# Softplus in a Mamba scan kernel: the rounding of 1+e moved from GpSimd to ScalarE, and all places in the order set anew

## What is computed

```python
dt = jax.nn.softplus(dbc[..., :DT_RANK] @ dt_proj_w.T + dt_proj_b)
A = -jnp.exp(A_log)
dA = jnp.exp(dt[..., None] * A)
dBu = dt[..., None] * Bm[:, :, None, :] * xs[..., None]
def combine(c1, c2):
    a1, b1 = c1
    a2, b2 = c2
    return (a1 * a2, a2 * b1 + b2)
_, hs = jax.lax.associative_scan(combine, (dA, dBu), axis=1)
y = jnp.einsum('blds,bls->bld', hs, Cm) + xs * Dvec
```

## Time and profile before

| what | value |
|---|---|
| median of 3 runs | 4836.43 us (4832.74 to 4845.68) |
| the profiled execution's own time | 4842.17 us |
| its span, first to last instruction | 4840.4 us |
| mean granted TensorE clock | 0.957 |
| instructions in the trace | 69756 |
| DMA moved | 623.06 MB, mean 129 GB/s |

### The profile page before, as it was taken

How to read it: one execution, slowest core, us unless ns; L and a number is a source line. 1 busy time by engine, 2 the same in 40 slices (tenths; PEclk the granted TensorE clock), 3 DMA queues, 4 the chain that set the end, 5 groups by cost and what they waited for, 6 DMA issues and landing times.

```text
span 4840.4 us, 69756 instructions
## 1 busy us (share of the span) xinstructions
PE 4236.6 (88%) x21206; PEld 1773.4 (37%) x21206; DVE 4002.3 (83%) x5617; ACT 3314.4 (68%) x5382; POOL 3939.5 (81%) x5162
## 2 busy tenths in 40 slices
PE   3578788999999999999989999999999989898897
PEld 1233333333333343434333434343333333333332
DVE  2268889888988888988898989888989898988872
ACT  1356566777777777777767776777777777676665
POOL 1268888888888888888888888888888889898873
PEclk9688899999999999999999999999999999999998
DMA  2366665656555665666656655666665665554430
GB/s 68 79 141 158 145 141 131 143 135 140 136 137 137 140 138 133 138 139 138 141 131 146 141 136 134 139 139 137 140 138 136 145 140 138 132 125 115 95 78 5
DMA packets 255529, 623.06 MB, mean 129 GB/s; under 512 B 105268, under 2 KB 170676, under 8 KB 255028
## 3 DMA queue, kind: packets, MB, share of 16 engines
q1 hardware_dynamic: 255156, 618.60, 55.8%
HBM read 540.85 MB, written 77.65 MB: 128 GB/s over the span
## 4 chain that ended last, share of the span: by engine, by line
POOL 35%; PE 24%; DVE 17%; issue 11%; DMA 7%; ACT 4%; SPq 0%; DVEq 0%; POOLq 0%; ACTq 0%
POOL hc L1156 14%; DVE hs L1011 7%; PE ps L676 5%; DMA dtb<-dt_scratch 5%; DVE ps L1001 4%; PE ps L740 3%; POOL sp L1169 2%; PE ps L689 2%; DVE tmpd L1070 2%; POOL h L1196 2%; POOL yw L1256 2%; PE ps L717 2%; POOL sp L1177 2%; PE ps L800 2%; PE ps L811 2%
## 5 line engine op out<-in xcount | busy, mean ns | idle before, releaser
L1156 POOL TENSOR_TENSOR hc<-hs,cb 128x448 f32<-128x448 f32 x1792 | 2025.6, 1137 | 460.5 <-DVE hs L1011 315.9
L1011 DVE TENSOR_TENSOR_SCAN hs<-dtb,state,ps 128x448 f32<-128x448 f32 x1536 | 1754.7, 1142 | 84.8 <-issue 0.7
L1001 DVE TENSOR_TENSOR ps<-ps,bb 128x448 f32<-128x448 f32 x1792 | 1099.1, 613 | 439.7 <-PE ps L676 437.9
L848 ACT ACTIVATE dtb<-dtb,decay 128x448 f32<-128x448 f32 x1792 | 1092.0, 658 | 156.0 <-DMA dtb<-dt_scratch 154.1
L676 PE MATMUL ps<-dux,pick 128*128 128x448 bf16 x3584 | 1038.1, 371 | 128.7 <-DVE hs L1011 117.1
L890 ACT ACTIVATE hg<-ps,be 128x448 f32<-128x448 f32 x896 | 523.8, 630 | 405.2 <-PE ps L740 404.6
L676 PE MATMUL ps<-duz,pick 128*128 128x448 bf16 x1792 | 642.5, 359 | 0.0
L676 PEld LDWEIGHTS ps<-dux,pick 128*128 128x128 bf16 x3584 | 283.7, 101 | 831.4 <-issue 432.1
L740 PE MATMUL ps<-xn,we 64*128 64x448 f32 x1792 | 564.5, 592 | 7.9 <-ACT hg L890 5.3
L879 ACT ACTIVATE rz<-ps,bnb 128x448 f32<-128x448 f32 x448 | 280.8, 627 | 271.4 <-PE ps L724 271.0
L689 PE MATMUL ps<-hc,gather 128*32 128x448 f32 x3584 | 451.3, 573 | 0.0
(11 more groups left out here) (171 smaller groups left out, 6319.3 us busy)
## 6 DMA issues: line engine op xcount, KB each, us to landing
dtb<-dt_scratch SPq DMA_DIRECT2D x448, 896.0 KB, 6.7
slab<-h_scratch SPq DMA_DIRECT2D x168, 290.0 KB, 8.3
dt_scratch<-sp SPq DMA_DIRECT2D x112, 224.0 KB, 2.0
...
xw<-xn_scratch SPq DMA_DIRECT2D x112, 112.8 KB, 2.7
xw<-xn_scratch SPq DMA_DIRECT2D x112, 112.5 KB, 3.7
```

Of the source, the lines that this page charges most:

```text
L848: A.activation(a, a, ACT.Exp, scale=decay[k % 2][:, i:i + 1]).then_inc(a_ok, 1)
L1001: V.tensor_tensor(bank, bank, bb[:, k % 2, :], ALU.mult).then_inc(bu_ok, 1)
L1011: V.tensor_tensor_scan(rev(hs[:, n % RH, :], d), rev(dtb[i // 4][:, i % 4, :], d), rev(bank, d), state[:, d, i:i + 1] if k % STEPS >= 2 el ...
L1156: P_.tensor_tensor(hc[:, n % 8, :], hs[:, n % RH, :], cb[:, k % 2, :], ALU.mult).then_inc(hc_ok, 1)
```

## The change

(1 + e) - 1 is made on ACT instead of on POOL, in two Identity operations (`lost`): y = 1 + e, and then 1 - y, which is the negative of what `soft_ym` made; `soft_log` adds it. y lies in the second half of dux, which the second part of dt·x overwrites later, so `lost` waits until PE has done with it (bu_ps). `soft_ym` is gone. The semaphore counts of the POOL chain follow. All places are set anew.

```diff
-AHEAD = 6
+AHEAD = 5
...
-'soft_le': -17, 'soft_ym': -17, 'soft_log': -15, 'soft_dt': -14, 'part0': -14, 'part1': -12
+'soft_le': -15, 'lost': -15, 'soft_log': -15, 'soft_dt': -14, 'part0': -9, 'part1': -5
...
+                def lost(kk):
+                    y = dux[:, kk % 2, 1, :]
+                    if kk >= 2:
+                        act.wait_ge(bu_ps, DS * (kk - 1))
+                    act.wait_ge(dt_e, kk + 1)
+                    A.activation(y, sp[:, 0, :], ACT.Identity, bias=1.0).then_inc(dt_y, 1)
+                    act.wait_ge(dt_y, kk + 1)
+                    A.activation(y, y, ACT.Identity, bias=1.0, scale=-1.0).then_inc(dt_r, 1)
...
-                def soft_ym(kk):
-                    pool.wait_ge(sp_ch, 3 * kk + 1)
-                    P_.tensor_scalar(sp[:, 0, :], sp[:, 0, :], 1.0, -1.0, ALU.add, ALU.add).then_inc(sp_ch, 1)
-
                 def soft_log(kk):
-                    pool.wait_ge(sp_ch, 3 * kk + 2)
-                    P_.tensor_tensor(sp[:, 2, :], sp[:, 2, :], sp[:, 0, :], ALU.subtract).then_inc(sp_ch, 1)
+                    pool.wait_ge(sp_ch, 2 * kk + 1)
+                    pool.wait_ge(dt_r, kk + 1)
+                    P_.tensor_tensor(sp[:, 2, :], sp[:, 2, :], dux[:, kk % 2, 1, :], ALU.add).then_inc(sp_ch, 1)
```

More of the change, by code:

```diff
@@ L61 @@
 END = NB * G
-STEP_AT = {'fetch_xw': -27, 'x': -20, 'silu_u': -20, 'dt': -17, 'soft_in': -17, 'bb': -12, 'copy_bb': -11, 'cc': -10, 'copy_cc': -9, 'z': -5, 'soft_le': -17, 'soft_ym': -17, 'soft_log': -15, 'soft_dt': -14, 'part0': -14, 'part1': -12, 'part2': -3, 'put_dt': -10, 'spread0': -5, 'spread1': -2, 'spread2': -2, 'spread3': 1, 'skip': 8, 'gather0': 9, 'gather1': 13, 'gather2': 15, 'gather3': 19, 'gate': 19, 'out_proj': 21, 'add_out': 21}
+STEP_AT = {'fetch_xw': -20, 'x': -20, 'silu_u': -20, 'dt': -17, 'soft_in': -17, 'bb': -12, 'copy_bb': -11, 'cc': -10, 'copy_cc': -9, 'z': -5, 'soft_le': -15, 'lost': -15, 'soft_log': -15, 'soft_dt': -14, 'part0': -9, 'part1': -5, 'part2': -3, 'put_dt': -8, 'spread0': -7, 'spread1': -2, 'spread2': 0, 'spread3': 2, 'skip': 8, 'gather0': 9, 'gather1': 13, 'gather2': 17, 'gather3': 19, 'gate': 19, 'out_proj': 21, 'add_out': 21}
@@ L63 @@
 UP_AT = (0, 0, 1, 1, 2, 2, 3, 3, 8, 8, 9, 9, 10, 10, 11, 11)
[L64 to L69, removed]
@@ L70 @@
-E_AT = {'mean': 1, 'square': 2, 'var': 2, 'power': 4, 'normed': 4, 'tokens_T': 9, 'logits': 10, 'compare': 12, 'places': 13, 'lead': 13, 'ask': 16, 'weigh': 19, 'share': 19, 'weights': 21, 'weight_parts': 21, 'parts': 25, 'fold': 49, 'out': 53}
+DOWN_AT = (4, 7, 12, 15)
+PAIR_AT = (3, 7, 12, 13)
+THIRD_AT = (0, 0, 1, 2, 2, 3, 5, 5, 6, 7, 7, 8, 10, 11, 12, 13)
+FOLD_AT = (4, 6, 7, 9, 11, 11, 14, 14, 14)
+A_AT = {'cut': -15, 'second': -10, 'put0': -10, 'rem1': -9, 'split1': -7, 'put1': -6, 'rem2': -8, 'split2': -6, 'put2': -6, 'arrange': -1, 'x_in': 10, 'paths': 14, 'mean': 16, 'square': 18, 'var': 19, 'power': 19, 'scaled': 20, 'normed': 23, 'norm_T': 24, 'keep_xn': 29}
@@ L71 @@
+F_AT = {'fetch': -4, 'x_T': 3, 'paths_in': 6, 'rows': 10}
+E_AT = {'mean': 0, 'square': 2, 'var': 2, 'power': 2, 'normed': 3, 'tokens_T': 9, 'logits': 10, 'compare': 12, 'places': 13, 'lead': 14, 'ask': 16, 'weigh': 20, 'share': 20, 'weights': 21, 'weight_parts': 21, 'parts': 27, 'fold': 49, 'out': 50}
 EXPERTS = 24
@@ L379, in build @@
         dtb_in = [sem(f"dtb_in{j}") for j in range(4)]
-        dt_e, dt_l, sp_ch, dt_ok, dx_ok = (sem(n) for n in ("dt_e", "dt_l", "sp_ch", "dt_ok", "dx_ok"))
+        dt_e, dt_l, dt_y, dt_r, sp_ch, dt_ok, dx_ok = (sem(n) for n in
+            ("dt_e", "dt_l", "dt_y", "dt_r", "sp_ch", "dt_ok", "dx_ok"))
         bu_ps, bu_ok, a_ok, h_ok, st_ok, hc_ok, y_acc, gated, o_ps, o_rd = (sem(n) for n in
@@ L979, in _ @@
                         soft_in(kk)
+                    for kk in steps_at(n, "lost"):
+                        lost(kk)
             @block.vector
@@ L1265, in _ @@
                         soft_le(kk)
-                    for kk in steps_at(n, "soft_ym"):
-                        soft_ym(kk)
                     for kk in steps_at(n, "soft_log"):
```

2 lines of the change are left out of this document (1 added, 1 removed).

## The result

The changed kernel takes **5023.55 us** (median of 4 runs, 5016.05 to 5040.95) against 4834.59 for the kernel before on the same chip (median of 4): a ratio of **1.0393**, 95% interval 1.0367 to 1.0418, 189 us slower. Forecast were 4824 us and a range of 4755 to 4910. The profiled execution took 5040.95 us, its span is 5038.9 us and its mean granted clock 0.938 (before 0.957). By 1 - clock that is 312 us of clock not granted, 104 us more than before.

What follows compares the result with a forecast made beforehand. DVE and PE were taken to bound alternating stretches of each period. Terms summed to -0.21 us per period, times 56 = -12 us, from 4842.17 to 4830; with the median 5.7 lower, 4824 us, range 4755 to 4910.

Steps and rivals of the forecast that it cites:

- What bounds: Per 32-slot period, DVE (96% busy) and PE (97%) limit alternate stretches; POOL is not the bound.
- Rival A: POOL was the bound after all, so one soft_ym per period counts in full: 96 us, 4740 us; chance 0.28.
- soft_ym, lost, keep_tokens: Per period: POOL's relief worth 0, two added ACT operations +0.55, less waiting of PE for xn -0.42 us.
- parts to 27: From slot 25: copy wT behind ACT's table load delays pair matmul L750 on the full PE, +1.41 us per period.
- Slot 19: PE's wait for acc leaves through moving a third, paths_in and share, but two folds stand there: -0.4 us per period.
- Folds: Slots 11 and 13 to 12 and 14: one fold leaves the part ahead of DVE's widest operation, -0.64 us per period.
- down: Slot 29 to 28: pair_out of slot 30 comes earlier, ending the wait of slot 31's down, -0.71 us per period.
- Rival B: Slots 27 to 4: wT and lost add up on ACT, no gains arrive: 4915 us, with all of lost 4979; chance 0.30.

Runs made afterwards that it cites:

- p_step: New operations with all places as before, plus only AHEAD 5 and the changed step places, gather2 left at 15: 4830.92 us, ratio 0.9981.
- the base: The change's new operations with all places as in the kernel before (lost at -15): 4822.76 us, ratio 0.9966 to the kernel before.

## Why the prediction was wrong

- **What bounds**: right, as far as POOL goes: taking 192 us off it gave 16 (9 to 24 by the interval). Rival A had 0.28 and is refuted by the operations alone (0.9966). The two windows of the earlier trace rows reach 0.9 us into the next period, which is 80.0 us long and not 80.9; nothing hangs on it.
- **soft_ym, lost, keep_tokens** (0, +0.55 and -0.42, together +0.13): measured together -0.3 us in a period. The wait for xn did end, but not through AHEAD: dt came earlier, which I had priced at 0. Of lost's half microsecond nothing shows by itself. Which of the three made how much was not measured.
- **parts to 27** (+1.41, upper end 1.41): this is the largest step that failed. The wait came true row by row, the size did not: 133 / 56 = 2.4. The wait is 1.1 of it. The 1.2 above that is the lower clock behind the wait. I had the row that shows such a fall, at slot 19, and used it only as a possible gain there; that a new wait brings a fall of its own was in no term and not in the range. The table load itself is 1.28 us and the copy stands 0.01 behind it; the Trainium skill, "ScalarE: Activation LUTs", section "What ACT_TABLE_LOAD costs", has 1.38 more for a drain, which these rows do not show.
- **gather2 to 17**: the step that failed by omission. It had no term. Alone it costs 66 us: the gather frees hc, hc holds up POOL, the softplus is late, and over the spread, the decay and xn PE waits. I had argued from eight hc buffers that what POOL releases is wanted slots later, and never asked what POOL waits for; the old trace had the row, 139.7 us of waits for gathers. The same chain, a late dt that holds up xn, was my term for keep_tokens. The moves of part0 and part1, which also had no term, cost little: p_step, with all step places but gather2's moved, lies 7 us above the base, which the noise can make.
- **Slot 19** (-0.4, ends +0.3 and -1.5): wrong in sign, and far outside its ends: +73 / 56 = 1.3. The wait for acc did leave and the clock did stay up there, but outb stood next in line, and the low clock moved to slots 20 to 22 with it. I had named paths_in's move as part of the gain, and it was the loss. The end of -1.5 was not the sum of its own row either: 3.6 us that hold 1.9 us of work lose 1.7.
- **Folds** (-0.64): wrong in sign, +0.3. I looked at the folds of slots 11 and 13 and not at the one that went from 17 to 19, behind the wait for acc.
- **down** (-0.71): right in kind, -0.5; the wait it was to end fell by 22.6 us of 39.8.
- **The sum.** One by one the measured parts make 5.2%: operations -0.3, down -0.5, folds 0.4, step places 0.15, parts 2.7, gather2 1.4, slots 16 to 20 1.5. Together, and with the small moves that are not in this list, they are 3.9%. The parts cover each other: in the changed kernel the place of parts costs 1.75%, with gather2 at 15 it costs 2.1%, alone 2.7%; slots 16 to 20 cost 0.7% with the changed tables around them, alone 1.5%.
- **Rival B** was the right side, and its price of 4915 to 4979 was still too low, since it came from the same 1.41 without the clock, without gather2 and without slots 16 to 20. Its gains did not stay away altogether: down's arrived in part.
